# A fused three-block network on one core: POOL rests during layer norms, contexts in halves, first stacks made earlier

## What is computed

```python
x = x + attn_a(layernorm(x))   # 16 heads of 64: softmax(q) per token, softmax(k) over tokens,
                               # context = q^T k per head, out = context * v, then w_out, b_out
x = x + ffn(layernorm(x))      # mu-mix with the previous token; sigmoid(r) * (relu(k)^2 @ W_v)
x = x + attn_b(layernorm(x))   # 16 heads of 8, rotary embedding, softmax(q k^T), then W_O
x = x + ffn(layernorm(x))      # the same feed-forward block again
```

## Time and profile before

| | |
|---|---|
| median of 3 runs | 1115.21 us (1114.8 to 1115.59) |
| the profiled execution | 1114.96 us, its span 1113.2 us |
| busy: PE, DVE, ACT, POOL | 949.8, 731.6, 674.6, 505.3 us |
| mean granted PE clock | 0.942 of full speed |
| filling steps | 0 to about 95 us |
| scores(0) of steps 3, 4, 15, 16 | 106.04, 171.81, 886.52, 944.97 us |
| scores(0) of step 17, draining | 997.99 us to the end |
| longest total waits of PE | ctx_wout's on qkv_sb 50.9; ffn_T's on h1T 19.4; first scores on a stack's DMA 10.8 |

### The profile page before, as it was taken

The page is one execution under the profiler, slowest core; times in us unless marked ns, Lnnn a source line. Parts: engine busy times, 40 slices in busy tenths (PEclk is TensorE's granted clock), DMA queues, the critical chain, the costliest instruction groups (busy, mean ns, idle before and its releaser), DMA issues.

```text
span 1113.2 us, 24352 instructions
## 1 busy us (share of the span) xinstructions
PE 949.8 (85%) x9835; PEld 541.9 (49%) x9835; DVE 731.6 (66%) x1542; ACT 674.6 (61%) x671; POOL 505.3 (45%) x346
## 2 busy tenths in 40 slices
PE   5995887997989899798989979898997999877983
PEld 3773544554545455454545545444554555433332
DVE  5675557577577867857786785778677666654233
ACT  4553655664756566475656646565664676656870
POOL 3657254544546444454645445464544545243100
PEclk9997988998989899898989989898998999998996
DMA  5003223123232312323231232323122131323210
GB/s 167 21 11 112 84 71 105 48 89 93 58 105 63 119 49 78 105 59 104 66 116 49 89 93 59 105 68 114 48 90 83 58 118 55 107 63 106 62 43 13
DMA packets 68667, 87.62 MB, mean 79 GB/s; under 512 B 13633, under 2 KB 40130, under 8 KB 68546
## 3 DMA queue, kind: packets, MB, share of 16 engines
q1 hardware_dynamic: 68546, 85.96, 25.5%
HBM read 16.19 MB, written 20.97 MB: 33 GB/s over the span
## 4 chain that ended last, share of the span: by engine, by line
PE 52%; DVE 22%; ACT 13%; issue 7%; SPq 2%; POOL 1%; DMA 1%; ACTq 0%; DVEq 0%
PE PS L1543 7%; ACT work L687 7%; PE PS L1587 7%; PE PS L1389 6%; DVE h L909 6%; PE PS L1457 5%; PE PS L1391 4%; PE PS L1390 4%; DVE hn L909 3%; DVE q_sum L951 3%; PE PS L1384 3%; PE PS L1501 3%; ACT work_b L687 3%; PE PS L1508 3%; PE PS L1478 2%
## 5 line engine op out<-in xcount | busy, mean ns | idle before, releaser
L687 ACT ACTIVATE work<-PS 128x2048 f32<-128x2048 f32 x150 | 281.6, 1877 | 134.6 <-PE PS L1543 134.6
L445 POOL TENSOR_TENSOR rs<-ve,half_neg 128x4 f32<-128x4 f32 x64 | 64.7, 1011 | 439.0 <-DVE ve L902 439.0
L677 ACT ACTIVATE work<-PS 128x512 f32<-128x512 f32 x256 | 152.8, 600 | 163.7 <-PE PS L1391 161.9
L687 ACT ACTIVATE work_b<-PS 128x2048 f32<-128x2048 f32 x74 | 138.9, 1877 | 68.8 <-PE PS L1543 68.8
L1587 PE MATMUL PS<-work,v 128*32 128x512 f32 x1368 | 179.4, 618 | 0.5 <-ACT work L694 0.5
L458 POOL TENSOR_TENSOR work<-work,q_rcp 128x1024 f32<-128x1024 f32 x64 | 121.8, 1903 | 83.5 <-DVE q_rcp L954 83.5
L1543 PE MATMUL PS<-q_st,k_st 32*128 32x512 f32 x896 | 118.1, 516 | 28.1 <-ACT work L687 11.8
L1389 PE MATMUL PS<-wqk,h1h 128*128 128x512 f32 x256 | 125.5, 490 | 5.7 <-issue 2.6
L1543 PEld LDWEIGHTS PS<-q_st,k_st 32*128 32x128 f32 x896 | 44.5, 188 | 143.8 <-ACT work L687 78.7
L1391 PE MATMUL PS<-wqk,h1l 128*128 128x512 f32 x256 | 102.3, 399 | 0.0
L951 DVE TENSOR_REDUCE q_sum<-work 128x16 f32<-128x1024 f32 x64 | 77.8, 1216 | 36.6 <-ACT work L677 36.4
(11 more groups left out here) (166 smaller groups left out, 1777.9 us busy)
## 6 DMA issues: line engine op xcount, KB each, us to landing
qkv_scratch<-qkv_sb SPq DMA_DIRECT2D x16, 768.0 KB, 4.4
rot<-qkv_sb SPq DMA_DIRECT2D x32, 256.0 KB, 2.4
k_st<-qk_hi SPq DMA_DIRECT2D x128, 64.0 KB, 2.1
k_st<-qk_lo SPq DMA_DIRECT2D x128, 64.0 KB, 2.1
q_st<-qk_hi SPq DMA_DIRECT2D x128, 64.0 KB, 2.1
q_st<-qk_lo SPq DMA_DIRECT2D x128, 64.0 KB, 2.1
parted<-U SPq DMA_DIRECT2D x52, 128.0 KB, 2.9
xa<-in_attn_a_x SPq DMA_DIRECT2D x16, 256.0 KB, 3.1
```

Of the source, the lines that this page charges most:

```text
L445: pool.tensor_tensor(rs[:, :], ve[:, :], half_neg[:, :], ALU.pow).then_inc(rstd[n].sem, 1)
L677: act.activation((EQ, EK)[r // 2][c % 2][:, (r % 2) * 512:(r % 2) * 512 + 512], PS[:, bank, :], ACT.Exp)\
L687: act.activation(probs_of(z, b, n), PS[:, 0:4, :], ACT.Exp).then_inc(z["s_exp"].sem, 1)
```

## The change

POOL gets a new wait, `rest_for_norm(n, j)`: it waits until all instructions of layer norm n of batch j are done on DVE. It stands behind the `rsqrt_var` of layer norms 0, 1 and 2 in the paired steps (behind `square` too for the last). `add_bias(s)` goes ahead of `rsqrt_var(0, a+1)`. On DVE `c_norm(s)` goes from ahead of `sums_of(a, 0)` to behind `ln1_norm(a+1)` where E holds, and `ln_norm(2, s)` from behind `sums_of(a, 3)` to ahead of it.

On PE contexts 1 and 2 are cut into two halves of 16 pairs each, and each half stands behind the weighings and ahead of scores(2k+1): context 1 in k = 5 and 6, context 2 in k = 7 and in k = 0 of the next step. Context 3 goes behind the weighings of k = 1, context 0 behind those of k = 4. The spacer is left out in paired steps.

In filling step 2 the pairs are swapped before xa and xr are loaded, POOL computes the rotary embedding and its split ahead of `rsqrt_var(1)` and `split_h1`, and the eight DMAs of the first stacks go out in two parts: four as soon as `qk_hi` is there, four when `qk_lo` is.

```diff
+            def first_stacks(z):
+                for part, rows in ((qk_hi, ((1, 0), (1, 2), (0, 0), (0, 1))), (qk_lo, ((1, 1), (1, 3), (0, 2), (0, 3)))):
+                    hold(sp, z["split"], 0, 1 if part is qk_hi else 2)
+                    for t, r in rows:
+                        stack, arrived = ((q_st, z["q_in0"]), (k_st, z["k_in0"]))[t]
+                        sp.dma_start(stack[0][r:P:4, :].bitcast(F32), part[0:32, t, :].bitcast(F32))\
+                          .then_inc(arrived.sem, 16)
...
+            def rest_for_norm(n, j):
+                hold(pool, ln[n], j)
...
@@ paired_step, POOL
                 if at_batch(i, 3):
                     rsqrt_var(2, l)
+                    rest_for_norm(2, l)
+                add_bias(s)
                 if there(a + 1):
                     rsqrt_var(0, a + 1)
-                add_bias(s)
+                    rest_for_norm(0, a + 1)
...
                 rsqrt_var(1, s)
+                rest_for_norm(1, s)
...
                     square(f2, e)
+                rest_for_norm(2, s)
                 if A:
                     q_hats(a, 3)
@@ paired_step, DVE
-                c_norm(s)
                 if not E:
+                    c_norm(s)
                     split_h3(l)
                 if A:
                     sums_of(a, 0)
                 if there(a + 1):
                     ln1_norm(a + 1)
                 if E:
+                    c_norm(s)
                     p_copy(l, 2)
...
+                ln_norm(2, s, x2, h3)
                 if A:
                     sums_of(a, 3)
-                ln_norm(2, s, x2, h3)
@@ paired_step, PE, between the weighings and scores(2k + 1)
+                    if k == 5 and A:
+                        hold(pe, ph_exp, a, 8)
+                        context_narrow(a, 1, range(0, 4))
+                    if k == 6 and A:
+                        context_narrow(a, 1, range(4, 8))
+                    if k == 7 and A:
+                        hold(pe, ph_exp, a, 12)
+                        context_narrow(a, 2, range(0, 4))
+                    if k == 0 and E and there(s):
+                        context_narrow(s, 2, range(4, 8))
+                    if k == 1 and E:
+                        hold(pe, ph_exp, s)
+                        context_narrow(s, 3)
                     scores(z, b, 2 * k + 1)
...
-                        ctx_wout(s)
+                        ctx_wout(s, spacer=False)
```

More of the change, by code:

```diff
@@ L339, in _ @@
             load_xa(1)
+            def first_stacks(z):
[5 more added lines that the diff above has]
+                          .then_inc(arrived.sem, 16)
             def filling_step(i, p):
                 a, s, l = i, i - 1, i - 2
+                if there(l):
+                    hold(sp, p_ev, l, 2)
+                    swap_pairs(att[0], l)
                 load_xa(a + 2)
@@ L345, in filling_step @@
                 if there(l):
-                    hold(sp, p_ev, l, 2)
-                    swap_pairs(att[0], l)
                     store_qkv(l)
-                    stack_k(att[0], l, 0)
-                    stack_q(att[0], l, 0)
+                    first_stacks(att[0])
                 if there(s):
@@ L554, in filling_step @@
                     rope_by_cos(att[0], l)
+                if there(s):
+                    rsqrt_var(1, s)
+                if there(l):
+                    rope_by_sin(att[0], l)
                 q_hats(a, 2)
                 if there(l):
-                    rope_by_sin(att[0], l)
                     rope_sum(att[0], l)
+                    split_qk(att[0], l)
                 split_h1(a + 1, 1 - p)
-                if there(l):
-                    split_qk(att[0], l)
                 q_hats(a, 3)
@@ L1448, in context, with context_narrow @@
                 mm.then_inc(c_mm.sem, 1)
-            def context_narrow(a, c):
+            def context_narrow(a, c, pairs=range(PAIRS)):
                 hold(pe, q_hat, a, c + 1)
-                for t in range(PAIRS):
+                for t in pairs:
                     for q in range(4):
@@ L1459, in context_narrow, with ctx_wout @@
                                        tile_position=(0, 32 * q), skip_group_check=True)
-                mm.then_inc(c_mm.sem, 1)
-            def ctx_wout(j, banks=(5, 7)):
+                if pairs[-1] == PAIRS - 1:
+                    mm.then_inc(c_mm.sem, 1)
+            def ctx_wout(j, banks=(5, 7), spacer=True):
                 pe.wait_ge(wout_in.sem, 16)
                 hold(pe, c_ev, j)
-                pe.matmul(PS[:, banks[0], 0:2], ident[:, :], ident[:, 0:2], start=True, stop=True)
+                if spacer:
+                    pe.matmul(PS[:, banks[0], 0:2], ident[:, :], ident[:, 0:2], start=True, stop=True)
                 for a in range(PAIRS):
@@ L1690, in paired_step @@
                         context_narrow(s, 3)
+                    if k == 1 and not E:
+                        hold(pe, f1["x"], s - 1, 1)
+                    if k > 0:
+                        weigh_values(z, b, 2 * k - 2, 1 - p)
+                        weigh_values(z, b, 2 * k - 1, 1 - p)
                     if k == 4 and A:
@@ L1771, in paired_step @@
                         h3_transposes(s)
[L1773 to L1781, removed]
             def draining_step(i, p):
```

2 lines of the change are left out of this document (removed).

## The result

The changed kernel takes 1005.19 us (median of 4 runs, 1004.03 to 1008.39) against 1115.01 (4 runs, 1113.89 to 1115.59): a ratio of 0.9021, 95% interval 0.8997 to 0.9044. The profiled execution is the one of 1004.03, its span 1002.2, its mean granted clock 0.983 (0.942 before).

What follows compares the result with a forecast made beforehand. PE, busy for 85% of the span, was taken as the bound, idling mostly at ctx_wout behind a norm slowed by POOL. Gains of 6.5 + 8.5 + 91.0 + 2.3 + 0.4 = 108.7 gave 1006.5 us, range 998 to 1015.

Steps and rivals of the forecast that it cites:

- Rivals 4 and 5: POOL is not why the norm is slow, 1092, chance 0.02; POOL's rests make its list set the step, 1155, chance 0.02.
- rival 2: Context halves on PE are not hidden in the gaps beside waiting scores; about 1021, chance 0.10.
- Rival 3: The last small waits in 12 steps go too, 10 more gained: 996; chance 0.08 for 990 to 998.
- Rival 1: A new wait at ctx_wout, from context 3, c_norm and the copy in one chain; 1025, chance 0.17.
- First stacks: In filling step 2, the new order brings the first scores 6.2 to 7.7 sooner, taken as 6.5 us.
- Step 3: PE's 4.54 wait for the slow norm goes, with lost clock and small terms: 8.5 us, between 5 and 10.
- Steps 4 to 14: Built from step 15 of before: 56.7 a step against 64.97, 91.0 us in all.
- wait of `ffn_T`: In paired steps, PE's wait there goes because its norm gets shorter: 1.20 a step.
- Step 15: The step without a batch to normalise gains from spacer, ffn_T's wait and halves, less cT's collision: 2.3 us.
- The collision of cT: DVE's product cT comes 4 us sooner and meets POOL's rope_sum: costs 0.3 a step, ends 0 and 0.5.
- The spacer: The small matmul ahead of ctx_wout on PE: leaving it out saves 0.31 a step, ends 0 and 0.31.
- Draining: The steps at the end of the kernel were taken to be as before: gain 0.

Runs made afterwards that it cites:

- e1: The kernel before with POOL's three rests and add_bias ahead of rsqrt_var alone; 1025.11 us, ratio 0.9192.
- e2: The changed kernel without POOL's rest instructions, all else as changed; 1089.78 us, ratio 0.9784.
- e9: The changed kernel without the rest for layer norm 0 of the next batch alone; 1068.34 us, ratio 0.9577.
- e10: The changed kernel without the rest for layer norm 1 alone; 1029.06 us, ratio 0.9217.
- e3: The changed kernel with contexts 1, 2 and 3 whole and at their old places; 1017.57 us, ratio 0.9137.
- e11: The changed kernel with rope_sum waiting for cT, and in step 17 a rest for layer norm 3, that norm ahead of pv_copy; 996.16 us.
- e12: The changed kernel with c_norm(s) back ahead of sums_of(a, 0) on DVE; 1020.94 us, ratio 0.9138.
- e4: The changed kernel with filling step 2's old order on POOL and SP; 1009.88 us, ratio 0.9057.
- e6: The changed kernel with one more wait on POOL: rope_sum waits for DVE's product cT; 1002.19 us, ratio 0.898.
- e7: The changed kernel with POOL resting for layer norm 3 in draining step 17 and that norm ahead of pv_copy on DVE; 998.93 us, ratio 0.8962.
- e5: The changed kernel with the spacer matmul back ahead of ctx_wout in paired steps; 1007.61 us, ratio 0.9034.

## Why the prediction was right, and where it was not

The forecast of 1006.5 stands 1.3 above the result, and the mechanism is the predicted one: e1, e2, e9 and e10 show that POOL's work beside the norms made them slow and that two rests take two waits away. The window of 150 to 780 us shows a clock of 1.00 and the norms `h<-xa` take 340 ns in the median. Rivals 4 and 5 fall with e1, rival 2 with e3. Rival 3's 990 to 998 was reached only with two more rests (e11). Rival 1, the new wait at `ctx_wout`, did not come, but e12 shows how near it lay: 1.41 of wait from the order of one DVE call.

- **First stacks**, 6.5, measured 5.81 (e4: 5.82). The wait fell by the predicted size, 10.82 to 4.40, which is 6.42. The step that failed is "Filling and draining steps are as before": PE reached the first scores 0.6 later.
- **Step 3**, 8.5, measured 9.17 in the profiled run. In e4, e6 and e7, with the same code in this step, it is 57.30, 58.25 and 58.57, in e5, with the spacer, 56.89, with granted clocks of 0.91 to 0.97. So part of this row is the clock of one run; 8.5 is as good as 9.17.
- **Steps 4 to 14**, 56.7, measured 56.35. Two terms were mis-sized and show in the result. The halves are worth 57.33 - 56.06 = 1.27 gross, not 1.07. And the 0.2 of wait at `ctx_wout` was counted twice: it already stood in step 15 of before, on which the sum was built. There too the spacer came 0.44 behind its forerunner (899.54 to 899.98). Together 0.4. Two more were off by as much and cancel, which is luck. The rests alone (e1) shorten step 15 from 58.45 to 57.45, so the wait of `ffn_T` was worth 1.00 there, not 1.20; and e1's steps 4 to 14 are only 0.16 longer than its step 15, where the sum has 0.35 for the four transposes.
- **Step 15**, 2.3, measured 2.53. No collision came there: the product started just ahead of POOL and took 0.69. The 1.00 for 1.20 takes two thirds of that back.
- **The collision of cT**, 0.3, measured 0.29 (e6). The Trainium skill, page "SBUF — State Buffer", section "Who interferes with whom", says that a DVE instruction with two SBUF inputs contends with GpSimd. The trace agrees: of the 13 products ten are stretched from 0.69 to about 2.8, and one, in step 16, to 2.16. The two that are not, in steps 4 and 15, took 0.77 and 0.69, so it did not come at every step. And the price at PE is 0.29, not the 0.5 that I worked out by it.
- **The spacer**, 0.31, was right by its row and wrong as a separate term: beside the collision it is worth 0.03 (e5), and the collision is worth 0.29 only because the spacer is gone. My sum took both, -0.31 and +0.3, and their net is what the kernel shows.
- **Draining**, 0, measured -1.83. `ln_norm(3, e)` of step 17 met POOL's rotary products before and after. PE waited 4.45 for it before and 6.09 after. The timelines show why. Before, POOL stood idle for 0.59 behind its third rotary product, waiting for a DMA, and the last two of the four norm instructions fitted into that gap (1026.45 to 1027.04). After, POOL stood idle for 0.17; it began its split at 913.83, the fourth norm instruction began at 913.93 and took 1.91. I had looked for the collision only where the change put a rest. In the kernels with this draining code the part takes between 114.5 and 119.1, so the 1.83 itself is not a firm figure.

The errors of the rows, +3.8 in steps 4 to 14 and +0.7 in step 3 against -0.7 at the first stacks and -1.8 in draining, partly cancel, which flatters the total.

The gain splits like this, by the steps' lengths: of the 8.62 a step, 7.12 are the rests when they are added last (e2), net of the collision of `cT` that came with them, and 1.50 halves and spacer. When the rests are added first (e1) it is 7.36 and 1.26.

## What to carry to other kernels

When DVE and POOL share a stretch, look at each DVE operation from SBUF to SBUF and compare its time with an undisturbed one; where a short chain on the critical path is stretched, one wait on POOL ahead of its long instruction buys it back, and POOL's idle time pays. Do it at every place where the two meet, filling and draining steps included. Before a small saving is added to a sum, see what else ends at the same point: a saving in one of two equal chains is worth nothing until the other goes too.

## What the runs showed of the hardware

Which engine loses goes by which starts first. Most of the time it was DVE. Beside `q_hats` and the two rotary products behind it the four norm instructions took 6.76 instead of 1.06, while `q_hats` took 1.903 in the mean before and 1.911 after, so POOL lost nothing there. But the product `cT` and POOL's `rope_sum` went either way. The changed kernel in steps 14 and 15:

```profile
736.72 2.38 POOL L489 TENSOR_TENSOR mask_cos<-mask_cos,rot 128x1024 f32<-128x1024 f32 x1
736.81 2.84 DVE L1101 TENSOR_TENSOR cT<-parted,cT 128x512 f32<-128x512 f32 x1
...
793.28 0.69 DVE L1101 TENSOR_TENSOR cT<-parted,cT 128x512 f32<-128x512 f32 x1
793.32 2.89 POOL L489 TENSOR_TENSOR mask_cos<-mask_cos,rot 128x1024 f32<-128x1024 f32 x1
```

In step 14 POOL starts 0.09 ahead and keeps its 2.38; in step 15 DVE starts 0.04 ahead and keeps its 0.69, and POOL takes 0.5 longer. e3, e4 and e5 have such pairs too (`rope_sum` at 2.7 to 2.9 where `cT` takes 0.69 to 0.87).

Not all of DVE's work is hit. The reciprocal of `cT` (one SBUF input) took 3.34 to 3.35 in every step, while POOL's rotary products ran beside it; copies and sums out of PSUM took their 0.69. Hit were, among others, the norm's tensor_scalar from SBUF to SBUF and the product with two SBUF inputs. Without rests the median norm instruction took 1.945 for 128x128 elements, about one instruction of POOL's (1.90 to 2.39). In e2 the second, third and fourth ended at 559.57, 561.92 and 564.23, each 0.08 to 0.09 behind an instruction of POOL's (559.49, 561.84, 564.14): POOL's next one had always started just ahead of DVE's. So each seems to wait for one POOL instruction to end. No run varied POOL's instruction length, so this last is read, not tested.
